# Second attention: where ScalarE applies a chunk's normalization among the copies of one batch

## Chip, cores and metric

One core of one Trainium2 chip runs the whole program as a single launch. The metric is the device time of an execution in microseconds (us); the time before is the median of three runs. All data are 32-bit floats.

## Reference, cut to what matters

The program is a chain of blocks on x of shape 32 x 128 x 128 (batch, token, feature): an attention, a recurrent feed-forward block, a mixture of experts feeding a second attention, and a slot-routing block. The change lies in the second attention. Per batch it computes

```python
# Q, K, V: relu projections of x (128 features = 16 heads of 8)
scores = einsum('bqhd,bkhd->bhqk', Qh, Kh) / sqrt(8)       # + causal mask, key mask
attn = softmax(scores, axis=-1) * query_mask
out = einsum('bhqk,bkhd->bqhd', attn, Vh).reshape(B, T, U) + x
mean, var = out.mean(-1), ((out - mean) ** 2).mean(-1)
normalized = (out - mean) / sqrt(var + 1e-8)
x_next = x_before + gamma * normalized + beta
```

After it, each batch is multiplied with a matrix of its own (a base matrix plus a rank-8 part) and added, and the slot block follows.

## The kernel before, in words

**Engines and order.** Each engine has its own list of instructions, written out by hand by a function of its own (`pe_attend2`, `act_attend2`, `dve_attend2`, `pool_attend2`, `sp_attend2`), and runs it in that order. Engines meet on semaphores alone: an instruction waits until a counter has reached a value. Nothing is reordered by a scheduler.

**Batches, units, chunks.** A batch q (0 to 31, `NB5` = 32) is one sequence of 128 tokens. Its 16 heads are handled as four units u = 4q to 4q+3 of four heads each (`U` = 128 units). A chunk c is four batches (512 tokens), 0 to 7. Each engine's function loops over q, and in iteration q it does, for batch q, the scores; for the four units of batch q-1, the turning of the probabilities; for batch q-2, the product with V. Four kinds of work form the path of a unit u:

- PE `pe_S5(q)` (L2113): 32-row score products of batch q, all 16 heads, into banks 0 to 3. It waits until the maxima of the batch before have read them.
- DVE `dve_max5(u)` (L2122): scale, mask and row maximum of a unit, to one of six buffers.
- POOL `pool_sub5(u)` (L2129): subtract the maximum, 128 x 512.
- ACT `act_exp5(u)` (L2134): exponential in place, 128 x 512.
- PE `pe_T5(u)` (L2141): four transposes of the exponentials into one bank.
- ACT `act_pt5(u)` (L2147): copy of that bank to one of eight buffers.
- PE `pe_PV5(q)` (L2158): 32 products of the turned probabilities with V; it waits for the copies of all four units. ACT `act_o5(q)` (L2165) copies the result, PE `pe_oT(q)` (L2171) turns it back, DVE `dve_norm5(q)` (L2180 to L2187) divides by the sums, POOL `pool_norm5(q)` (L2194) adds x, DVE `dve_stats5(q)` (L2199, L2201) takes mean and variance.

Work of a chunk as a whole stands between these, at hand-chosen steps. A step s runs from 0 to 127, four to each q; `aside(s)` says what belongs to step s, and each engine's loop picks its part of it. For chunk c with finished statistics: `pool_root5` (L2325 to L2330, root and mean on POOL), `act_apply5` (L2336, four activations of 128 x 128 in place, one per batch: scale and shift of the normalization), `pe_gamma5` (L2343, four transposes), `dve_gamma5` (L2349), `pe_select5` and `pe_add5` with their DVE parts. `FINISH` holds the offset of each from `LATE` + 16c; `PROJECT` holds the projections of a later chunk (`act_query5`, L1629, and `act_key5`, L1641, on ACT).

**Banks of PE's outputs.** The turned probabilities of the units ("p"), the product with V ("o") and the query and key projections ("q", "k") share banks 4 and 5 in turn. `plan5` lays the turn down in PE's order, and `pe_drained5` makes an entry wait for the copy of the entry two before it:

```python
        def pe_drained5(key):
            first, n = through5[key]
            if n >= 2:
                pe.wait_ge(*drained5[first][n - 2])
```

With the order of one iteration, "p" 4q-4, "p" 4q-3, "o" q-2, (projection), "p" 4q-2, "p" 4q-1, this means: where there is no projection, `pe_T5(4q-1)` waits for `act_o5(q-2)`; the next iteration's `pe_T5(4q)` and `pe_T5(4q+1)` wait for `act_pt5(4q-2)` and `act_pt5(4q-1)`.

**ScalarE's order.** One iteration of `act_attend2` issues: exp 4q-1, copy 4q-4, copy 4q-3, asides of steps 4q and 4q+1, exp 4q, `act_o5(q-2)`, aside of 4q+2, exp 4q+1, aside of 4q+3, copy 4q-2, exp 4q+2, copy 4q-1. The apply of chunk c stands at step 29 + 16c, in iteration q = 4c + 7, for c = 0 to 6 (chunk 7's stands in `OPENING` of the last stage). POOL does the root of chunk c at the end of its iteration 4c + 6, ahead of `pool_norm5` and `pool_sub5(4q)` of iteration 4c + 7; PE turns the applied chunk (`pe_gamma5`) in iteration 4c + 8. Below, "iteration 7 + 4c" is the iteration of chunk c's apply.

Of the kernel before, what the change touches and what calls it, by code (L numbers as in the profile page):

```python
# [58 lines left out]
def build(nc, xT_d, w_d, out_d):  # L59
# [4 lines left out]
    with ctx:  # L64
# [1928 lines left out]
        LATE = 28  # L1993

        PROJECT = {2: "query", 6: "key", 7: "keysum", 8: "tokens", 11: "masks"}
        FINISH = {0: "root", 1: "apply", 4: "gamma", 14: "select", 18: "add"}

        def aside(s):

# [9 lines left out]
            if s == 26:  # L2009
                yield "b1", 0  # L2010
            for i, what in FINISH.items():
                c, i = divmod(s - LATE - i, 16)
# [10 lines left out]
        def plan_aside(what, c):  # L2023
            if what == "query":
                passes5(("q", c), 4, s_qt, c + 1)
            if what == "key":
                passes5(("k", c), 4, s_kt, c + 1)
            if what == "keysum":
                passes5(("ks", c), 6, s_kx, c + 1)
            if what == "tokens":  # L2030
                passes5(("x", c), 6, s_xc, c + 1)
            if what == "b1":
                passes5("b1", 6, s_b1, 3)
            if what == "factors":
                passes5(("f", c), 6, s_facd, c + 1)
            if what == "gamma":
                passes5(("T", c), 6, s_fd, 3 * c + 1)
            if what == "select":
                passes5(("A", c), 6, s_fd, 3 * c + 2)
            if what == "add":  # L2040
                passes5(("B", c), 6, s_fd, 3 * c + 3)
# [15 lines left out]
        def plan5():  # L2057
# [26 lines left out]
            plan_aside("add", 6)  # L2084
            for what in FINISH.values():
                plan_aside(what, 7)
# [1158 lines left out]
```

## Time and profile before

| | |
|---|---|
| runs, us | 955.38, 953.97, 954.27 (median 954.27) |
| the profiled execution, us | 953.82 |
| its span, us | 952.2 |
| outside the span, us | 1.6 |
| mean granted clock of PE | 0.996 |
| second attention, from its first scores to its last copy | about 645 to 865 us of the span |

Times in the rows are microseconds from the start of the span. PE is TensorE's products, PEld its weight loads, DVE VectorE, ACT ScalarE, POOL GpSimd. L2336 is line 2336 of the kernel. A row of a timeline merges neighbouring instructions of one line ("x4"): start, time from the first start to the last end, engine, line, operation, tiles, and in brackets how long the engine had been idle and which instruction released it. Instructions of one engine overlap a little in the records, so that the next one's start lies before the recorded end; idle time is counted from that end. PB are PE's output banks, AR_s the working area that holds all tiles of this stage.

### The profile page before, as it was taken

To read this page: it belongs to the slowest core of one execution; us is meant where nothing else is said; L and a number is where in the kernel's file an instruction comes from. 1 tells how busy PE (TensorE), PEld (TensorE's weight loads), DVE (VectorE), ACT (ScalarE), POOL (GpSimd) and SP (SyncE) were. 2 spreads that over 40 slices of the span, in tenths; PEclk is the share of its full clock that TensorE was granted. 3 is DMA by queue.
4 is the path that set the end of the run, shared out by engine and by line. 5 is a ranking of instruction groups with operands and counts; after the bars stand their busy time and mean duration, and the time that the engine had idled before them with its cause. 6 is when DMAs were issued, how large, how long until landed. Compare 5 with 4: busy or idle time off the path is not lost.

```text
span 952.2 us, 25813 instructions
## 1 busy us (share of the span) xinstructions
PE 914.9 (96%) x8641; PEld 733.2 (77%) x8641; DVE 790.5 (83%) x3563; ACT 794.7 (83%) x2162; POOL 547.2 (57%) x670
## 2 busy tenths in 40 slices
PE   8999999999999999999989999999989999999887
PEld 7899989898989989963326888867877777775566
DVE  6766989989898989989996767658889889896985
ACT  7998989898989888867875989987788888886886
POOL 4444636464564646442795157757789888891041
PEclk9999999999999999999999999999999999999899
DMA  9100000000000000000236898911000000000002
GB/s 370 71 2 2 2 2 2 2 2 2 1 2 2 2 1 2 2 2 0 91 134 193 275 318 288 328 49 32 24 20 18 24 17 21 24 3 1 2 1 89
DMA packets 36226, 57.70 MB, mean 61 GB/s; under 512 B 3456, under 2 KB 27264, under 8 KB 35712
## 3 DMA queue, kind: packets, MB, share of 16 engines
q1 hardware_dynamic: 36096, 56.07, 17.4%
q8 instruction: 69, 1.13, 0.5%
q14 instruction: 61, 0.50, 0.2%
HBM read 40.85 MB, written 11.01 MB: 54 GB/s over the span
## 4 chain that ended last, share of the span: by engine, by line
PE 54%; DVE 18%; ACT 7%; issue 4%; POOL 3%; DMA 1%; SPq 1%; DVEq 0%; ACTq 0%; POOLq 0%
PE PB L2141 6%; PE PB L270 4%; PE PB L271 4%; PE PB L272 4%; PE PB L437 3%; PE PB L2113 3%; PE PB L2158 3%; PE PB L390 2%; PE PB L459 2%; DVE W L400 2%; PE PB L1423 2%; DVE AR_s L349 2%; PE PB L1425 2%; PE PB L1424 2%; DVE HFXT L607 2%
## 5 line engine op out<-in xcount | busy, mean ns | idle before, releaser
L409 ACT ACTIVATE W<-W,small 128x128 f32<-128x128 f32 x384 | 149.1, 392 | 12.1 <-DVE small L400 11.3
L421 POOL TENSOR_TENSOR W<-W,small 128x512 f32<-128x512 f32 x96 | 100.6, 1053 | 100.2 <-DVE small L415 100.2
L270 PE MATMUL PB<-RR_s 128*128 128x256 f32 (+1 forms) x468 | 151.7, 324 | 5.7 <-DVE RR_s L471 3.8
L271 PE MATMUL PB<-RR_s 128*128 128x256 f32 (+1 forms) x468 | 139.9, 299 | 0.0
L272 PE MATMUL PB<-RR_s 128*128 128x256 f32 (+1 forms) x468 | 139.7, 298 | 0.0
L2129 POOL TENSOR_TENSOR AR_s<-AR_s,small 128x512 f32<-128x512 f32 x128 | 129.8, 1043 | 15.6 <-DVE small L2122 15.5
L2122 DVE CUSTOM_DVE_ANT_0 AR_s<-PB,W 128x128 f32<-128x128 f32 x512 | 111.3, 287 | 2.2 <-PE PB L2113 0.3
L1399 DVE TENSOR_TENSOR RR_s<-AR_s,RR_s 128x512 fp32r<-128x512 f32 (+1 forms) x96 | 65.5, 687 | 44.6 <-ACT RR_s L1392 40.8
L270 PEld LDWEIGHTS PB<-RR_s 128*128 128x128 f32 x468 | 88.8, 190 | 16.0 <-DVE RR_s L471 6.4
L400 DVE CUSTOM_DVE_ANT_0 W<-PB,W 128x128 f32<-128x128 f32 x384 | 86.0, 282 | 13.6 <-PE PB L390 12.8
L349 DVE COPY AR_s<-PB 128x512 f32<-128x512 f32 x128 | 84.8, 682 | 13.2 <-PE PB L272 13.1
L271 PEld LDWEIGHTS PB<-RR_s 128*128 128x128 f32 x468 | 89.1, 190 | 3.4 <-issue 0.7
L272 PEld LDWEIGHTS PB<-RR_s 128*128 128x128 f32 x468 | 88.8, 190 | 3.0
L2134 ACT ACTIVATE AR_s<-AR_s 128x512 f32<-128x512 f32 x128 | 79.7, 625 | 10.6 <-POOL AR_s L2129 10.1
L2147 ACT ACTIVATE AR_s<-PB 128x512 f32<-128x512 f32 x128 | 72.5, 592 | 17.9 <-PE PB L2141 17.6
L443 ACT ACTIVATE HFXT<-PB 128x512 f32<-128x512 f32 x123 | 73.0, 594 | 14.4 <-PE PB L437 11.0
L2141 PEld LDWEIGHTS PB<-W,AR_s 128*128 128x128 f32 x512 | 56.5, 141 | 26.5 <-issue 12.3
L2141 PE MATMUL PB<-W,AR_s 128*128 128x128 f32 x512 | 70.9, 278 | 5.2 <-ACT AR_s L2165 2.7
L1457 POOL TENSOR_TENSOR HFXT<-HFXT,AR_s 128x128 f32 x68 | 41.1, 633 | 56.8 <-DVE AR_s L1447 56.7
L409 ACT ACTIVATION_READ_ACCUMULATOR W<-W,small 128x1 f32 x384 | 73.3, 191 | 0.0
L390 PE MATMUL PB<-AR_s 64*128 64x128 f32 x1024 | 65.8, 278 | 0.0
L1392 ACT ACTIVATE RR_s<-AR_s 128x512 fp32r<-128x512 f32 (+1 forms) x96 | 57.3, 597 | 8.5
(461 smaller groups left out, 2637.6 us busy)
## 6 DMA issues: line engine op xcount, KB each, us to landing
RR_s<-W1D SPq DMA_DIRECT2D x13, 512.0 KB, 4.2
RR_s<-W2D SPq DMA_DIRECT2D x13, 512.0 KB, 4.6
W<-in_w SPq DMA_DIRECT2D x1, 5895.5 KB, 24.3
RR_s<-XD SPq DMA_DIRECT2D x46, 128.0 KB, 3.1
XD<-RR_s SPq DMA_DIRECT2D x18, 256.0 KB, 3.6
HQ<-W1D SPq DMA_DIRECT2D x6, 512.0 KB, 4.3
HQ<-W2D SPq DMA_DIRECT2D x6, 512.0 KB, 4.9
HQ<-XD SPq DMA_DIRECT2D x22, 128.0 KB, 3.5
```

Source lines behind the costliest of these rows:

```text
L270: nc.tensor.matmul(out, lh, rh, start=True, stop=False)
L271: nc.tensor.matmul(out, ll, rh, start=False, stop=False)
L272: return nc.tensor.matmul(out, lh, rl, start=False, stop=True)
L349: nc.vector.tensor_copy(QK[v % 2][pr], bank("k", n)[:, :]).then_inc(s_qk, 1)
L390: mm = nc.tensor.matmul(score(u, h), qk[r, b * 128:b * 128 + 128], qk[r, 256 + b * 128:256 + b * 128 + 128], start=True, stop=True)
L400: nc.vector.tensor_tensor_reduce(SS[r][:, hl], score(u, h), w("mask"), -0.125, 3.0e38, ALU.add, ALU.min, mx[r][:, h:h + 1]).then_inc(s_max, 1)
L409: e = nc.scalar.activation(SS[r][:, hl], SS[r][:, hl], ACTF.Exp, bias=mx[r][:, h:h + 1], scale=-1.0, accum_out=rc[r][:, h:h + 1])
L421: nc.gpsimd.tensor_tensor(s3, s3, over(rc[r], 2, [128, 4, 128]), ALU.mult).then_inc(s_nrm, 1)
L2122: nc.vector.tensor_tensor_reduce(SS5[r][:, hl], score5(u, h), w("mask"), isq8, -3.0e38, ALU.add, ALU.max, mx5[r][:, h:h + 1]).then_inc(s_m ...
L2129: nc.gpsimd.tensor_tensor(s3, s3, over(mx5[r], 2, [128, 4, 128]), ALU.subtract).then_inc(s_sub, 1)
L2134: nc.scalar.activation(SS5[r], SS5[r], ACTF.Exp).then_inc(s_ex5, 1)
L2141: mm = nc.tensor.transpose(bank5(("p", u))[:, hl], SS5[u % 6][:, hl], ident)
```

## The change

The step of "apply" goes from 29 + 16c to 30 + 16c. In `act_attend2` it then falls to the pick at step 4q+2, which stands behind `act_exp5(4q)` and `act_o5(q-2)` of the same iteration and ahead of `act_exp5(4q+1)`. Seven chunks (0 to 6) are touched. No instruction is added or dropped, no wait is changed, no other engine's order changes, and "apply" takes no turn in the banks, so `plan5` lays down the same turns. Chunk 7's apply stays.

```diff
         PROJECT = {2: "query", 6: "key", 7: "keysum", 8: "tokens", 11: "masks"}
-        FINISH = {0: "root", 1: "apply", 4: "gamma", 14: "select", 18: "add"}
+        FINISH = {0: "root", 2: "apply", 4: "gamma", 14: "select", 18: "add"}
```

## Rows read from the trace of the kernel before

**Rows 1.** Page, busy us (share of the span) and instructions
```profile
PE 914.9 (96%) x8641; PEld 733.2 (77%) x8641; DVE 790.5 (83%) x3563; ACT 794.7 (83%) x2162; POOL 547.2 (57%) x670
```

**Rows 2.** Stretches: bounds, length, busy us per engine, granted clock, DMA
```profile
720.50:747.00 26.50, 25.86 (x365) 20.00 (x364) 23.64 (x164) 22.58 (x45) 23.02 (x33) 1.00 0.09 22
```

**Rows 3.** Timeline of PE: start, us, engine, line, what, count, [idle <-releaser]
```profile
697.40 0.65 PE L2141 MATMUL PB<-W,AR_s 128*128 128x128 f32 x4 [1.92 <-ACT AR_s L2165]
...
699.53 1.09 PE L2141 MATMUL PB<-W,AR_s 128*128 128x128 f32 x8
...
726.05 1.09 PE L2141 MATMUL PB<-W,AR_s 128*128 128x128 f32 x8
726.98 0.60 PE L2343 MATMUL PB<-W,AR_s 128*128 128x128 f32 x4
...
727.73 1.08 PE L2158 MATMUL PB<-AR_s 128*32 128x128 f32 x32
...
835.72 0.66 PE L2141 MATMUL PB<-W,AR_s 128*128 128x128 f32 x4 [0.32 <-ACT AR_s L2165]
...
841.38 0.66 PE L2141 MATMUL PB<-W,AR_s 128*128 128x128 f32 x4 [0.44 <-ACT AR_s L2165]
...
853.69 1.29 PE L2141 MATMUL PB<-W,AR_s 128*128 128x128 f32 x8
```

**Rows 4.** Timeline of ACT, round the apply of chunks 0 and 1
```profile
694.70 1.65 ACT L2336 ACTIVATE AR_s<-AR_s,small 128x128 f32<-128x128 f32 x4 [0.54 <-POOL small L2330]
696.25 0.61 ACT L2134 ACTIVATE AR_s<-AR_s 128x512 f32<-128x512 f32 x1
...
698.77 0.58 ACT L2147 ACTIVATE AR_s<-PB 128x512 f32<-128x512 f32 x1
...
721.22 1.65 ACT L2336 ACTIVATE AR_s<-AR_s,small 128x128 f32<-128x128 f32 x4 [0.19 <-POOL small L2330]
722.78 0.61 ACT L2134 ACTIVATE AR_s<-AR_s 128x512 f32<-128x512 f32 x1
723.30 0.57 ACT L2165 ACTIVATE AR_s<-PB 128x512 f32<-128x512 f32 x1
723.77 0.62 ACT L2134 ACTIVATE AR_s<-AR_s 128x512 f32<-128x512 f32 x1
...
725.29 0.58 ACT L2147 ACTIVATE AR_s<-PB 128x512 f32<-128x512 f32 x1
...
728.39 0.63 ACT L2134 ACTIVATE AR_s<-AR_s 128x512 f32<-128x512 f32 x1 [0.56 <-POOL AR_s L2129]
```

**Rows 5.** Timeline of POOL, the subtraction (L2129) behind the root
```profile
695.03 1.04 POOL L2129 TENSOR_TENSOR AR_s<-AR_s,small 128x512 f32<-128x512 f32 x1
...
721.55 1.04 POOL L2129 TENSOR_TENSOR AR_s<-AR_s,small 128x512 f32<-128x512 f32 x1
...
727.31 1.05 POOL L2129 TENSOR_TENSOR AR_s<-AR_s,small 128x512 f32<-128x512 f32 x1 [0.43 <-DVE small L2122]
...
851.95 4.05 POOL L2129 TENSOR_TENSOR AR_s<-AR_s,small 128x512 f32<-128x512 f32 x4
```

**Rows 6.** Waits, 640 to 880: total us, times, longest us
```profile
DVE small L2180 <- PE PB L2171: 15.5, 23, 1.2
...
ACT AR_s L2336 <- POOL small L2330: 5.6, 8, 3.8
...
PE PB L2141 <- ACT AR_s L2165: 2.7, 3, 1.9
```

**Rows 7.** Busy time by stretch, two stretches in the closing stage
```profile
890.00:894.30 4.30, 4.30 (x24) 3.40 (x21) 3.67 (x23) 1.85 (x6) 0.00 (x0) 0.50 0.00 0
894.30:900.00 5.70, 5.22 (x37) 3.42 (x36) 5.27 (x31) 4.95 (x14) 0.00 (x0) 1.00 0.00 0
```

**Rows 8.** Timeline of PE in the closing stage, L2649 twice
```profile
889.24 1.99 PE L2649 MATMUL PB<-AR_s 128*64 128x129 f32 x16
...
896.62 1.10 PE L2649 MATMUL PB<-AR_s 128*64 128x129 f32 x16 [0.48 <-ACT AR_s L2631]
```

## The prediction, made before the changed kernel ran

> **What bounds the kernel now.** First the page's busy times: PE is busy for 96% of the span, every other engine for less [rows 1]. That is an average, so next the stretches round the applies. The applies of chunks 0 to 4 start 26.5 us apart, and the stretch of one such period shows PE busy 25.86 of 26.50 us, POOL 23.02, ACT 22.58, at a granted clock of 1.00; the three periods behind it repeat these figures [rows 2]. PE is therefore the bound of this stage, and whatever stops PE here is paid in full, since its list has nothing to catch up with. Third, PE's timeline: the reader looks for brackets, stretches in which PE had run dry. Of the transposes L2141 that waited for the copy of the product (`act_o5`, L2165) there are three, 2.7 us together [rows 6]: 1.92 us in iteration 7, where chunk 0's apply stands, and 0.32 and 0.44 us in iterations 28 and 29, where none stands [rows 3]. In iterations 11, 15, 19 and 23 PE does not wait for that copy at all. So what the edit can free at most is seen at once: the stall in iteration 7, once, and some hundredths in iteration 31.
>
> Fourth, ACT and POOL side by side round an apply. ACT is idle when the apply's root comes, 0.54 us at chunk 0 and 0.19 at chunk 1 [rows 4]; over the stage that wait is 5.6 us, of which 3.8 belong to chunk 7, which is not touched [rows 6]. Then it runs the four activations, and takes up exp 4q. POOL in that time adds one batch and subtracts the maximum for exp 4q: 695.03 + 1.04 = 696.07 at chunk 0, 721.55 + 1.04 = 722.59 at chunk 1 [rows 5]; exp 4q starts at 696.25 and 722.78 [rows 4]. **The apply fills a hole**: it runs while exp 4q's operand is still being made, and exp 4q comes only 0.14 us later than it could (0.04 us from POOL's end to ACT's start, as where exp 48 waits for POOL: 727.31 + 1.05, then 728.39 [rows 4, 5]).
>
> **The change, part by part.** It removes and adds no instruction, and touches no DMA and no queue but ACT's. It moves four activations, seven times, behind exp 4q and `act_o5`.
>
> *What comes earlier.* exp 4q and `act_o5` by 0.14 us each, not by the 1.56 us of the apply (721.22 to 722.78 [rows 4]), for POOL's subtraction is late next. Iteration 7: `act_o5` ends 0.14 us earlier, so PE's second half of the transposes starts at about 697.26 instead of 697.40. That only matters if nothing holds PE behind it.
>
> *What comes later.* With chunk 1's times: exp 44 at 722.63, `act_o5` 0.52 later at 723.15 (722.78 to 723.30 [rows 4]), the apply 0.47 later at 723.62, its 1.56 us, exp 45 at 725.18 instead of 723.77. From there ACT's list runs with its old spacing and 1.42 us late: copy 43 starts at 725.29 + 1.42 = 726.71 and ends 0.58 us later, at 727.29 [rows 4]; copy 42, one copy and one exponential (1.00 us) ahead, ends at 726.29.
>
> *Who waits for that.* The next iteration's transposes: T 44 goes to the bank of 42, T 45 to the bank of 43. They ran at 726.05 as eight in a row [rows 3], the second four from about 726.54 (four of its spacings of 0.12 us). With 0.05 us from ACT's end to PE (as 696.77 + 0.57, then 697.40, from the row of L2165 beside [rows 3]), T 44 can start at 726.34, 0.3 us late, and T 45 at 727.34, **0.80 us late**. Behind T 45 stand, on PE, gamma (726.98), a V product, PV (727.73 [rows 3]) and all that follows.
>
> *Is more lost, or some won back?* PV also needs copy 43 (727.29, before 728.53: free) and bank turn of copy 44 (about 728.3: free). `pe_gamma5` needs the apply, now done at 725.3 and used at 727.8: free, covered by 2.5 us; that is the cover of the apply's own lateness. The next batch's subtraction ends at 728.36 [rows 5], ACT comes to it at 728.7, 0.3 late, and `act_o5` then waits for PV anyway. DVE's `dve_gamma5` slips by some 0.4 us, into the hole in which DVE waits for PE at the head of the next iteration (DVE waits for L2171 23 times, 15.5 us [rows 6]). Since DVE, and behind it POOL, take up each iteration from PE's L2171, both slip by the same 0.80 us, and at the next apply the engines stand to each other as before. So the price is not paid once but at each apply.
>
> *Chunk 0:* copy 27 started at 698.77 [rows 4]; 698.77 + 1.41 + 0.58 + 0.05 = 700.81, against T 29 at 699.53 + 0.49 = 700.02 [rows 3]: 0.79 late, and the 0.14 us won ahead of it are swallowed. *Chunks 1 to 4:* 4 x 0.80 = 3.2. *Chunk 5* (iteration 27): 0.80 again, but iterations 28 and 29 have the stalls of 0.32 and 0.44 us, where PE waits for a chain over DVE and POOL that starts ahead of the delay. Of the 0.80 they take up all but what PV itself and `dve_gamma5` carry on, which I put at 0.27. *Chunk 6* (iteration 31): the next transposes come only after the set-up products and a hidden layer, at 857.5, copies 122 and 123 would end at 856.7 and 857.7, and the second is needed by PV at 858.1: nothing lost. exp 124's subtraction ends at 851.95 + 1.04 = 852.99 [rows 5]; the transposes at 853.69 took 1.29 us instead of 1.09, so they held a short wait for `act_o5` [rows 3], which goes: about 0.15 won, leaving 0.12 for chunks 5 and 6 together.
>
> **Sum:** 0.79 + 3.20 + 0.12 = 4.1 us more. The last stage takes it over whole: PE runs on without a gap until 880, where DVE begins to lead, starting from PE's products. Against the profiled execution (953.82, of which 952.2 are the span): 957.9 us. The median of the runs stands 0.45 above that execution: 954.27 + 4.1 = **958.4 us**. Bounds of the price at one apply: 0.3 us, if only T 44's wait counted and T 45 were hidden; 1.42 us, ACT's whole slip, if some further wait had no slack. I take 0.80 since both times in it come from rows a microsecond apart.
>
> **Rivals.** *1. Faster: the stall goes.* Mechanism: `act_o5(5)` is freed of the apply's 1.56 us ahead of it. For it: PE's longest stop of the stage is just this wait [rows 3, 6]. It decides by exp 4q's operand: POOL would have to be done when ACT is free, at about 694.2, not at 696.07; and the copies behind must not bind. Then 1.6 us from iteration 7 and 0.2 from iteration 31 are won: 952.5 us. The rows of POOL speak against it, and ends on POOL are said to be rough, but the same kind of end released ACT within 0.04 us at 728.39. 7%. *2. No change.* The late copies fall into PE's slack. It decides by the 0.64 us of each period in which PE isn't busy: if these were at T 44 and T 45, the price is near nothing, 954.3 us. They are elsewhere (most of it behind the projection's copy in iteration 12). 9%. *3. Half.* DVE and POOL run ahead while PE stands, the next subtraction is early, and ACT's hole shrinks; or only part of the wait counts: 2.1 us, 956.4. Against it: they wait for PE in each iteration. 7%. *4. More.* The stops reach `act_o5` or the projection behind them, near 1.2 us each, five times: 960.3 us. 5%. *5. The clock.* In the closing stage 890 to 894.3 ran at a granted 0.50, the level of 1.2 GHz, its neighbour at 1.00, 2.4 GHz [rows 7]; it had fallen in a part of the stage where PE stops again and again. The same 16 products took 1.99 us at the lower and 1.10 at the higher level [rows 8], some 1.5 us over that whole stretch. If the new stops bring such a fall into this stage, or one more in the last, 1.5 us come on top: 959.9. Against it: the stop of 1.92 us in iteration 7 left the clock at 1.00. 5%.
>
> The Trainium skill speaks for case 5, in "TensorE: Matmul & The Clock Gate", section "Part 4: PE-mode transpose": a transpose does not count as PE being busy in the way a product does. By that rule a stage so full of transposes is near the lower level already, and new stops could tip it: the sum would be 4.1 us and the price of the lower level on top, 959.9. The granted 1.00 of rows 2, with twenty transposes in each iteration of it (`pe_T5`, `pe_oT`), disagrees so far.
>
> That the edit does nothing is no case: ACT's order is its list.
>
> **How the numbers follow.** Forecast 67%, range of its own 957.4 to 959.4 (0.6 to 1.0 us per apply). With the half case at the low end and the added cases at the high end, 956.2 to 960.3 holds 84%. About 0.2% (1.9 us) is what a measurement can tell: slower takes the forecast, 3, 4 and 5, 0.84; same 0.09; faster 0.07.
>
> **What would show it.** In the changed profile: ACT idle before exp 4q for 1.4 us in iterations 7, 11, ... by L2129; `pe_T5` with two brackets, 0.3 and 0.5, by L2147, in iterations 8, 12, 16, 20, 24, 28; applies 27.3 us apart; no 1.92 us stop. I am wrong if exp 4q starts before POOL's recorded end, or if the applies stay 26.5 us apart.

## The result, and the profile after

| | before | changed |
|---|---|---|
| median of 6 runs, us | 954.83 | 958.78 |
| lowest to highest, us | 953.97 to 956.16 | 958.47 to 960.03 |
| profiled execution, us | 953.82 | 958.89 |
| its span, us | 952.2 | 957.6 |

The changed kernel is slower: the ratio of the runs is 1.0038, with a 95% interval of 1.0023 to 1.0053, so 2.2 to 5.1 us. The forecast was 958.4, 4.1 us more. The two profiled executions lie 5.1 us apart. (One of the 17 runs of the kernel before beside experiments 5 to 8 took 1262.23 us at a mean granted clock of 0.653 and is left out of their ratios.)

The page's busy times, where one sees that nothing was added: PE 1.9 us more busy than in [rows 1], ACT 1.4 less, on a span 5.4 us longer. The instruction counts are the same; what grew is mostly PE's idle time, and its 1.9 us of busy time are looked at below.

```profile
PE 916.8 (96%) x8641; PEld 734.5 (77%) x8641; DVE 791.2 (83%) x3563; ACT 793.3 (83%) x2162; POOL 548.0 (57%) x670
```

Next ACT's timeline round chunk 1's apply (columns as in [rows 4]).

```profile
721.29 1.08 ACT L2147 ACTIVATE AR_s<-PB 128x512 f32<-128x512 f32 x2 [0.44 <-PE PB L2141]
723.98 0.63 ACT L2134 ACTIVATE AR_s<-AR_s 128x512 f32<-128x512 f32 x1 [1.60 <-POOL AR_s L2129]
724.51 0.58 ACT L2165 ACTIVATE AR_s<-PB 128x512 f32<-128x512 f32 x1
724.99 1.64 ACT L2336 ACTIVATE AR_s<-AR_s,small 128x128 f32<-128x128 f32 x4
726.53 0.62 ACT L2134 ACTIVATE AR_s<-AR_s 128x512 f32<-128x512 f32 x1
...
728.05 0.58 ACT L2147 ACTIVATE AR_s<-PB 128x512 f32<-128x512 f32 x1
```

And POOL's subtraction for exp 44, the first of four (compare [rows 5]).

```profile
722.90 4.05 POOL L2129 TENSOR_TENSOR AR_s<-AR_s,small 128x512 f32<-128x512 f32 x4
```

This is what the prediction described. ACT ends its two copies at 722.38 and now stands idle for 1.60 us until POOL's first subtraction ends, at 722.90 + 1.04 = 723.94; exp 44 starts 0.04 us later. The apply no longer fills that hole. It comes behind the copy of the product, and copy 43 starts at 728.05, which is 5.15 us after the subtraction's start, where it was 725.29 - 721.55 = 3.74 before [rows 4, 5]: 1.41 us late. Over the stage, the waits by kind (who <- for whom: total, times, longest):

```profile
ACT AR_s L2134 <- POOL AR_s L2129: 18.1, 17, 1.9
...
DVE XF L2349 <- PE PB L2343: 6.4, 8, 2.1
...
PE PB L2141 <- ACT AR_s L2147: 2.9, 10, 0.3
...
PE PB L2141 <- ACT AR_s L2165: 2.4, 3, 1.8
```

ACT waits 18.1 us for the subtraction, where the trace before had 10.1. And PE now waits for L2147, the copies, ten times, twice at each of five applies; before, that row did not exist. PE's timeline, with the places that answer to [rows 3]:

```profile
697.15 0.66 PE L2141 MATMUL PB<-W,AR_s 128*128 128x128 f32 x4 [1.79 <-ACT AR_s L2165]
...
698.17 1.93 PE L2113 MATMUL PB<-KR,QS 32*128 32x128 f32 x32
700.03 1.94 PE L2141 MATMUL PB<-W,AR_s 128*128 128x128 f32 x8
701.79 0.61 PE L2343 MATMUL PB<-W,AR_s 128*128 128x128 f32 x4
...
706.56 1.17 PE L2113 MATMUL PB<-KR,QS 32*128 32x128 f32 x32
...
727.68 0.66 PE L2141 MATMUL PB<-W,AR_s 128*128 128x128 f32 x4 [0.24 <-ACT AR_s L2147]
728.69 0.66 PE L2141 MATMUL PB<-W,AR_s 128*128 128x128 f32 x4 [0.35 <-ACT AR_s L2147]
729.18 0.60 PE L2343 MATMUL PB<-W,AR_s 128*128 128x128 f32 x4
...
841.20 0.66 PE L2141 MATMUL PB<-W,AR_s 128*128 128x128 f32 x4 [0.19 <-ACT AR_s L2165]
...
846.83 0.66 PE L2141 MATMUL PB<-W,AR_s 128*128 128x128 f32 x4 [0.40 <-ACT AR_s L2165]
...
859.14 1.17 PE L2141 MATMUL PB<-W,AR_s 128*128 128x128 f32 x8
```

The stops of 0.24 and 0.35 us stand at the transposes of units 44 and 45, in iteration 12. The second ran 1.01 us after the first, where it followed at once before. The stops by L2165 of 1.92, 0.32 and 0.44 us are 1.79, 0.19 and 0.40 now: little came back, as little was to come. Two rows are new in kind: 698.17 and 700.03, 32 score products in 1.93 us and eight transposes in 1.94 us, where the same work takes 1.17 and 1.09 elsewhere (row 706.56, and row 699.53 of [rows 3]). The stretches say why, and give one whole period of the steady part (columns as in [rows 2]):

```profile
698.20:701.50 3.30, 3.30 (x40) 3.08 (x40) 2.26 (x15) 3.26 (x8) 2.25 (x5) 0.53 0.02 5
...
728.00:755.30 27.30, 26.09 (x366) 19.95 (x364) 23.66 (x164) 22.40 (x44) 22.97 (x33) 1.00 0.09 21
```

PE's granted clock was 0.53 on the mean from 698.2 to 701.5, that is the lower level of 1.2 GHz for nearly all of it, right behind the stop of 1.79 us. In the steady part one period of the applies is 27.35 us; the stretch above, 27.30 us long, has PE busy for 26.09 of it, where it was 25.86 of 26.50 [rows 2].

**Where the time came from.** The starts of gamma's transposes (L2343) mark PE's progress, chunk by chunk; a row of four small products (L2308) at 689.40 (689.28 in the changed kernel), ahead of the first apply, gives the origin. The table holds the distance from one mark to the next.

| stretch of PE's list | before, us | changed, us | difference | forecast |
|---|---|---|---|---|
| origin to gamma 0 | 11.06 | 12.51 | +1.45 | +0.79 |
| gamma 0 to gamma 4, four periods | 106.02 | 109.45 | +3.43 | +3.20 |
| gamma 4 to gamma 5 | 26.49 | 27.35 | +0.86 | +0.80 |
| gamma 5 to gamma 6 | 27.60 | 27.31 | -0.29 | -0.68 |
| gamma 6 to gamma 7 | 13.28 | 13.28 | 0 | 0 |
| sum | 184.45 | 189.90 | +5.45 | +4.1 |

The stage took 5.45 us more, which is all that the span grew by. The medians of the runs lie only 3.95 us apart, and the interval of the timed difference ends at 5.1. Runs of one kernel scatter by 0.7 to 5.3 us from lowest to highest, and part of that arises ahead of this stage: the origin mark lay between 688.57 and 693.24 us in the ten traces of this case. Within the steady part the marks are the finer measure: the four periods agree within 0.03 us in the trace before and within 0.04 in the changed one. At chunk 0 they compare single executions, and there the granted clock differs between them (the trace of the kernel before has no fall in this stage). So the experiments below are read by both, and the sum of the stage with care wherever its first entry holds such a fall.

### The profile page after: what moved, and what is told of

Same layout as the page of the kernel before. It is cut to its first block, busy times and chain, and to the rows that moved or that the text cites. A ratio compares the mean times of both kernels' runs of the same rounds, so it can differ in the third digit from the quotient of the medians.

```text
span 957.6 us, 25813 instructions
## 1 busy us (share of the span) xinstructions
PE 916.8 (96%) x8641; PEld 734.5 (77%) x8641; DVE 791.2 (83%) x3563; ACT 793.3 (83%) x2162; POOL 548.0 (57%) x670
## 4 chain that ended last, share of the span: by engine, by line
PE 49%; DVE 17%; ACT 10%; POOL 7%; issue 5%; DVEq 0%; ACTq 0%; POOLq 0%
PE PB L270 5%; PE PB L271 4%; PE PB L272 4%; PE PB L437 4%; PE PB L2141 3%; POOL AR_s L2129 3%; PE PB L390 3%; PE PB L459 2%; PE PB L2158 2%; DVE W L400 2%; PE PB L1423 2%; PE PB L1425 2%; PE PB L1424 2%; PE PB L2113 2%; ACT W L409 2%
## 5 line engine op out<-in xcount | busy, mean ns | idle before, releaser
L2129 POOL TENSOR_TENSOR AR_s<-AR_s,small 128x512 f32<-128x512 f32 x128 | 129.8, 1043 | 19.7 <-DVE small L2122 19.7
L2134 ACT ACTIVATE AR_s<-AR_s 128x512 f32<-128x512 f32 x128 | 79.9, 626 | 18.5 <-POOL AR_s L2129 18.1
L443 ACT ACTIVATE HFXT<-PB 128x512 f32<-128x512 f32 x123 | 73.1, 594 | 14.5 <-PE PB L437 11.5
L2147 ACT ACTIVATE AR_s<-PB 128x512 f32<-128x512 f32 x128 | 72.5, 592 | 15.0 <-PE PB L2141 14.6
```

The lines of the kernel that those rows point to most:

```text
L2129: nc.gpsimd.tensor_tensor(s3, s3, over(mx5[r], 2, [128, 4, 128]), ALU.subtract).then_inc(s_sub, 1)
L2134: nc.scalar.activation(SS5[r], SS5[r], ACTF.Exp).then_inc(s_ex5, 1)
```

## The experiments

Eight experiments ran, the last of them the changed kernel itself once more. Theory H is the prediction's: the apply filled ACT's hole ahead of exp 4q; once moved, it pushes the two copies behind it past the point where PE needs their banks, anew at each apply. Its rivals were that the cost is paid once ("paid once"), that the apply is late for gamma (G), and that ACT's longer wait is itself the price (W). "Stage" is the distance from the origin mark to gamma 7 in the kernel's trace, less the 184.45 us of the kernel before.

**Experiment 1: chunk 0 alone.**

```diff
             for i, what in FINISH.items():
+                i += what == "apply" and s < LATE + 16
```

(on the kernel before)

> Only chunk 0's apply is moved; chunks 1 to 6 keep the old place. Theory H (the apply filled ACT's hole before exp 4q; moved, the copies behind it are late and PE waits at the two transposes of the next iteration, anew at each apply): 0.8 us over the kernel before, or 1.4 if PE's granted clock falls to half behind the stop of iteration 7 as in the changed kernel's profile; applies of chunks 1 to 4 stay 26.5 us apart. Rival 'paid once' (the move shifts the engines against each other for good): most of the 4 us, 3 to 4 us over the kernel before.

Measured: 954.51 us against 954.31 for the kernel before beside it, ratio 1.0001 (0.9991 to 1.0010). Stage +1.49 us. PE's timeline (lines shifted by one: L2142 is `pe_T5`, L2114 the scores):

```profile
696.44 0.66 PE L2142 MATMUL PB<-W,AR_s 128*128 128x128 f32 x4 [1.79 <-ACT AR_s L2166]
...
697.46 1.92 PE L2114 MATMUL PB<-KR,QS 32*128 32x128 f32 x32
699.31 1.95 PE L2142 MATMUL PB<-W,AR_s 128*128 128x128 f32 x8
...
851.51 1.08 PE L2159 MATMUL PB<-AR_s 128*32 128x128 f32 x32 [0.34 <-ACT AR_s L2148]
```

The applies of chunks 1 to 4 are 26.5 us apart again. From the fourth row, which was at 850.86 us before, against an origin 0.83 us earlier: the 1.48 us lost at chunk 0 are still there at the end, no more and no less. "Paid once" would have 3 to 4 us and is out. The trace shows the larger value of H, with the lower clock (1.92 and 1.95 us for the scores and the transposes); the timed runs show 0.2 us with a bound of 1.0. The two differ by more than I can explain from one trace; part of it lies behind the stage, where this trace spent 3.4 us at the lower clock in place of 6.8. Nor does the trace show the two waits of H at chunk 0: the eight transposes of iteration 8 run without a gap, the copies they need ending at 698.92 and 699.92 us. The 1.48 us are the lower clock's, so this experiment speaks against "paid once", and for a price that is gone wherever the apply is back in its old place, but it has no measure of what late copies cost.

**Experiment 2: behind exp 4q only, ahead of the product's copy.**

```diff
                 act_exp5(4 * q)
+                step_of({"apply": act_apply5}, 4 * q + 1)
                 ...
                     act_o5(q - 2)
```

(on the kernel before, with "apply" taken out of the table of asides)

> All seven applies stand behind exp 4q but still ahead of the copy of the turned outputs' product (act_o5). Theory H: ACT waits for the subtraction as in the changed kernel, and act_o5 comes 1.4 us later than before, so PE waits for it at transpose 4q-1 in the same iteration: 1.4 us per chunk instead of 0.86, about 9 us over the kernel before (8 to 10), and little or no wait for the copies of 4q-2 and 4q-1. Rival G (the price is that the apply itself is late for gamma on PE and DVE): the apply is done 1 us earlier than in the changed kernel, so the price is less than its 4 us.

Measured: 964.62 against 954.31, ratio 1.0104 (1.0084 to 1.0123); stage +11.5. ACT, then PE:

```profile
725.70 0.63 ACT L2134 ACTIVATE AR_s<-AR_s 128x512 f32<-128x512 f32 x1 [1.61 <-POOL AR_s L2129]
726.24 1.63 ACT L2336 ACTIVATE AR_s<-AR_s,small 128x128 f32<-128x128 f32 x4
727.78 0.57 ACT L2165 ACTIVATE AR_s<-PB 128x512 f32<-128x512 f32 x1
```

```profile
728.41 0.66 PE L2141 MATMUL PB<-W,AR_s 128*128 128x128 f32 x4 [1.22 <-ACT AR_s L2165]
...
865.96 0.65 PE L2141 MATMUL PB<-W,AR_s 128*128 128x128 f32 x4 [1.46 <-ACT AR_s L2165]
```

The same hole of 1.6 us, then the apply, and `act_o5` is the late one: PE stops 1.22 us for it at each apply, and not once for a copy. The applies are 27.93 us apart, 1.43 more than before, as H had it; the total of 10.3 us by the medians is a little over the 8 to 10 expected. G is out: counted from exp 4q's start the apply ends at 2.17 us, where it was 2.65 in the changed kernel, so it is 0.48 us earlier (not 1 us, as the expectation had it), and yet the price of a period is 1.43 us in place of 0.86. What was left out of the expectation is the stop of 1.46 us in iteration 31.

**Experiments 3 and 4: the root behind POOL's first subtraction, with either place of the apply.**

```diff
                     pool_sub5(4 * q)
+                    step_of({"root": pool_root5}, 4 * q)
                     pool_sub5(4 * q + 1)
                 ...
-                step_of({"root": pool_root5}, 4 * q + 4)
```

> The changed kernel with POOL's root behind its first subtraction of the iteration (pool_sub5(4q), then root, then pool_sub5(4q+1)). Theory H: exp 4q finds its operand 1.8 us earlier and the long stop of PE in iteration 7 shrinks to 0.3 us or less, but then the apply waits for the root and the copies behind it are late by 0.5 us at the transposes: about 956 us, 2 us over the kernel before and 2 to 3 under the changed one. Rival G: the root and so the apply come 1.1 us later still, so slower than the changed kernel, 960 or more.

> The kernel before (apply ahead of exp 4q) with the same late root on POOL. Theory H: now the apply holds exp 4q and act_o5 instead of filling a hole; act_o5 2.1 us later in a steady iteration, 1.5 us in iteration 7: about 11 us over the kernel before. With this order on POOL the move of the apply would pay 9 us, where with the old order it costs 4. Rival (the move is bad whatever POOL does, because of the order of copies): this kernel stays ahead of e3.

Measured: 959.73 us in the new place (ratio 1.0059, 1.0042 to 1.0077; stage +6.5) and 981.15 in the old one (1.0286, 1.0264 to 1.0308; stage +27.5), beside 954.31. Between the two, the direction is H's: with the root late, moving the apply pays 21 us, while with the root early it costs 4 to 5. Both sizes were missed, and for experiment 3 so was the direction against the changed kernel: H had it 2 to 3 us faster, and it is not (5.4 us over the kernel before, periods of 27.69 us in place of 27.35), with a long stop in iteration 7 of 1.09 us and not 0.3. By its time alone rival G, with "960 or more", came nearer; but G's wait, gamma's transposes for the apply, does not occur on PE in this trace: each of its new stops is for a copy. POOL, ACT and PE of experiment 3:

```profile
720.89 0.46 POOL L2194 TENSOR_TENSOR AR_s<-AR_s 128x128 f32<-128x128 f32 x1 [0.93 <-DVE AR_s L2187]
721.65 1.04 POOL L2129 TENSOR_TENSOR AR_s<-AR_s,small 128x512 f32<-128x512 f32 x1 [0.31 <-DVE small L2122]
```

```profile
722.73 0.63 ACT L2134 ACTIVATE AR_s<-AR_s 128x512 f32<-128x512 f32 x1 [0.99 <-POOL AR_s L2129]
...
724.67 1.65 ACT L2336 ACTIVATE AR_s<-AR_s,small 128x128 f32<-128x128 f32 x4 [0.82 <-POOL small L2330]
```

```profile
727.37 0.66 PE L2141 MATMUL PB<-W,AR_s 128*128 128x128 f32 x4 [0.56 <-ACT AR_s L2147]
728.37 0.66 PE L2141 MATMUL PB<-W,AR_s 128*128 128x128 f32 x4 [0.34 <-ACT AR_s L2147]
```

POOL, freed of the root, now waits 0.93 us for DVE's norm and 0.31 for DVE's maxima before it may subtract. **The root, too, had filled a hole.** Moving it behind the subtraction made that one only 0.6 us earlier relative to ACT's copies (a wait of 0.99 us in place of 1.60), and then the apply waited 0.82 us for the root. So copy 43 starts 7.09 us after the pair of copies ahead of exp 44, against 6.76 in the changed kernel, and the period is 27.69 us. In experiment 4 ACT and PE show:

```profile
727.76 1.65 ACT L2336 ACTIVATE AR_s<-AR_s,small 128x128 f32<-128x128 f32 x4 [2.93 <-POOL small L2330]
```

```profile
730.46 1.12 PE L2141 MATMUL PB<-W,AR_s 128*128 128x128 f32 x4 [2.54 <-ACT AR_s L2165]
731.37 1.06 PE L2171 MATMUL PB<-W,AR_s 128*128 128x128 f32 x4
732.36 1.82 PE L2113 MATMUL PB<-AR_s,W 32*128 32x128 f32 x32
```

ACT waits 2.93 us for the root with everything queued behind it, PE stops 2.54 us at each apply, and the clock is at its lower level behind each such stop (32 scores in 1.82 us): the trace has a stretch of 3.4 us at 0.50 behind each of the six stops. The period is 30.75 us, 4.25 more than before, which is about the stop of 2.54 us and half of the 3.4 us at the lower level (an estimate from these rows, as PE is busy for 3.34 of them): I had counted the later root against an idle POOL and no clock. By the same estimate some 10 of the 21 us between experiments 3 and 4 are the clock's.

**Experiment 5: two activations of the four.** The two others, and with them the normalization of the first two batches of chunks 0 to 6, are left out.

```diff
-            for b in range(4):
+            for b in (range(4) if c == 7 else (2, 3)):
```

> The changed kernel with only two of the four activations of the apply for chunks 0 to 6; the first two batches of those chunks are left unnormalized. Nothing else moves, ACT still waits 1.4 to 1.6 us for the subtraction ahead of exp 4q. Theory H (the price is what the apply adds behind that wait, less the slack of the two transposes): 0.78 us less in front of the copies, so they are late by 0.64 and not 1.42 us, just inside the slack: no stops of PE by L2147, applies 26.5 us apart, 954 us, that is within 1 us of the kernel before and 4 under the changed one. Rival W (the wait of ACT for the subtraction is itself the price): the wait is there in full, so 4 us stay, 958.5.

Measured: 955.25 against 954.89 beside it, ratio 1.0004 (0.9993 to 1.0015); stage +0.39. ACT:

```profile
726.57 0.63 ACT L2134 ACTIVATE AR_s<-AR_s 128x512 f32<-128x512 f32 x1 [1.60 <-POOL AR_s L2129]
727.10 0.58 ACT L2165 ACTIVATE AR_s<-PB 128x512 f32<-128x512 f32 x1
727.58 0.86 ACT L2336 ACTIVATE AR_s<-AR_s,small 128x128 f32<-128x128 f32 x2
728.35 0.61 ACT L2134 ACTIVATE AR_s<-AR_s 128x512 f32<-128x512 f32 x1
...
729.87 0.58 ACT L2147 ACTIVATE AR_s<-PB 128x512 f32<-128x512 f32 x1
```

The wait for the subtraction is there in full, 1.60 us, but PE has no stop by L2147 at all, and the applies are 26.60 us apart. W is out: ACT's waiting costs PE nothing by itself; what stands behind it does. Copy 43 starts 729.87 - 726.53 = 3.34 us after the subtraction's end, against 2.70 before and 4.11 in the changed kernel: it is 0.64 us late, and PE pays 0.1 for it.

**Experiment 6: six activations.**

```diff
             act.wait_ge(s_fl, 4 * c + 4)
+            for b in (0, 1) if c < 7 else ():
+                q = 4 * c + b
+                nc.scalar.activation(place(14592 + 256 * c + 128 * b, 128), cs(LN[c % 2], b, 128), ACTF.Identity, ...)
```

> The changed kernel with six activations in the apply of chunks 0 to 6 (two more, whose results go to an unused place). Theory H: beyond the slack every microsecond is paid in full, so each of the two activations of 0.385 us costs PE 0.77 us per chunk together: transposes stop 1.6 us per apply instead of 0.86, applies 28.1 us apart, about 5 us over the changed kernel, 964 us. Rival W: unchanged, 958.8.

Measured: 963.44 against 954.89, ratio 1.0094 (1.0078 to 1.0111); stage +11.9. This trace has 6.8 us at the lower clock from 698.3 us on, and the stage's sum holds it: 2.0 us up to gamma 0, and 29.57 us for the next period where the following ones take 28.12. PE, in iteration 16:

```profile
758.29 0.66 PE L2141 MATMUL PB<-W,AR_s 128*128 128x128 f32 x4 [0.99 <-ACT AR_s L2147]
759.29 0.66 PE L2141 MATMUL PB<-W,AR_s 128*128 128x128 f32 x4 [0.35 <-ACT AR_s L2147]
```

The applies are 28.12 us apart. So the period is 26.60, 27.35 and 28.12 us with two, four and six activations, of which each pair is 0.77 us: the first pair falls for the most part into the slack, and the second and the third cost PE 0.75 and 0.77 us. The copies are late by 0.64, 1.41 and 2.18 us and PE by 0.10, 0.86 and 1.62, so that the slack at the second group of transposes is about 0.55 us in all three.

**Experiment 7: the apply behind the copies.**

```diff
                     act_pt5(4 * q - 1)
+                step_of({"apply": act_apply5}, 4 * q + 2)
```

(on the changed kernel, with "apply" taken out of the table of asides)

> The apply stands at the very end of ACT's iteration, behind the copies of 4q-2 and 4q-1. Theory H: the two stops of PE by L2147 at the transposes go. What is late next: gamma's transposes, which need the apply (0.3 us), and the product with V, whose bank needs the copy of 4q, now behind the apply (0.4 us): about 0.65 us per chunk, applies 27.15 us apart, 957 to 958.5 us. Rival G (the apply's lateness for gamma is the price in the changed kernel): the apply is now 2 us later still, so the price grows to over 2 us per chunk, 966 or more.

Measured: 957.90 against 954.89, ratio 1.0036 (1.0024 to 1.0049); stage +4.7, of which 1.4 up to gamma 0, where the clock was at its lower level again. PE in iteration 12:

```profile
727.54 1.09 PE L2141 MATMUL PB<-W,AR_s 128*128 128x128 f32 x8
728.95 0.63 PE L2343 MATMUL PB<-W,AR_s 128*128 128x128 f32 x4 [0.31 <-ACT AR_s L2336]
729.41 0.39 PE L2207 MATMUL PB<-W,HFXT 128*128 128x128 f32 x2
729.95 1.08 PE L2158 MATMUL PB<-AR_s 128*32 128x128 f32 x32 [0.15 <-ACT AR_s L2147]
```

The eight transposes run through in 1.09 us again. In their stead gamma waits 0.31 us for the apply and the product with V 0.15 for a copy; the applies are 27.22 us apart. H's next-in-line waits are the ones that came, and the period is 0.72 us longer than before, where H had 0.65. G is out here too: the apply is later than in the changed kernel, and the price is lower. Each of the three places behind exp 4q that were tried costs something; with the apply in the hole ahead of it, PE has no stop in iterations 11 and 12 but the one for the projection (L1629), which all of these kernels have.

**Experiment 8: the changed kernel again.**

> The changed kernel once more, beside the others: 4 to 4.5 us over the kernel before. It tells whether PE's granted clock falls to half behind the stop of iteration 7 again: if so, chunk 0's gamma is 1.45 us late and the other chunks' 0.86 each, if not, chunk 0's too is 0.8 to 0.9.

Measured: 959.06 against 954.89, ratio 1.0053 (1.0034 to 1.0072); stage +5.4, with 12.48 us from the origin to gamma 0 (12.51 above) and the same stops in the same places:

```profile
756.72 0.65 PE L2141 MATMUL PB<-W,AR_s 128*128 128x128 f32 x4 [0.23 <-ACT AR_s L2147]
757.72 0.66 PE L2141 MATMUL PB<-W,AR_s 128*128 128x128 f32 x4 [0.35 <-ACT AR_s L2147]
```

The clock was at the lower level again in iteration 8. Together with the first comparison the move costs about 4 to 5 us (3.95 and 4.17 by the medians, 3.6 and 5.1 by the ratios).

## Why the prediction was right, and which terms were off

- **The hole.** The prediction read from [rows 4, 5] that the apply ran while POOL was still making exp 4q's operand, so that exp 4q would gain 0.14 us and not 1.56. Measured: exp 4q starts 0.04 us after the subtraction, and the stop of 1.92 us only shrank to 1.79. Right.
- **The copies.** Forecast late by 1.42 us; measured 1.41. Right.
- **The two stops of PE.** Forecast 0.3 and 0.5 us in iterations 8, 12, ..., 28; measured 0.24 and 0.35 as recorded idle time, in 12, 16, 20, 24 and 28; idle time is counted from the modelled end of the products before, and by the starts, counted from the start of the iteration's 32 scores, T 44 comes at 1.41 us in place of 1.11 and T 45 at 2.42 in place of 1.60, so 0.3 and 0.8 us late. Right in place and kind in these five; in iteration 8 neither stop came (see chunk 0). Experiments 5 and 6 show that the length of the apply behind the wait is what is paid, past 0.55 us of slack, and experiment 2 that the waits move to `act_o5` when the apply stands ahead of it.
- **The price per apply.** Forecast 0.80, measured 0.86 (27.35 against 26.49). The term left out that a group of four transposes takes PE longer right behind a stop: gamma's follow the second group's start by 729.18 - 728.69 = 0.49 us, where the second four of eight in a row take 0.44 (726.54 to 726.98 before).
- **Anew each time.** Right: four periods alike, and experiment 1 took the price away wherever the move was undone.
- **Chunks 5 and 6.** Forecast 0.12 together, measured 0.86 - 0.29 = 0.57. This is the step that was off. It held that the stops in iterations 28 and 29, of 0.32 and 0.44 us, would take up most of the delay, since the chain over DVE starts ahead of it. It put 0.53 us on them; by the starts of PE's rows they took up 0.14 in iteration 28 and 0.03 in iteration 29, and iteration 31 gave back 0.12 where 0.15 was forecast. In iteration 28 the chain over DVE and POOL is indeed ready early, but another one ends last in its place: `act_o5` waits for PE's own product with V, which is as late as PE is.

```profile
840.55 0.60 ACT L2165 ACTIVATE AR_s<-PB 128x512 f32<-128x512 f32 x1 [0.50 <-PE PB L2158]
```

Some 0.19 us of the stop therefore stays however late PE comes: it is 0.18 or 0.19 in experiments 3, 6, 7 and 8 as well, whose delays differ. In iteration 29 almost nothing is taken up (0.40 us of stop left of 0.44): that chain starts with DVE's maxima of batch 29, and these wait for the scores, which stand in PE's list behind the late transposes. The trace has the first maximum 0.41 us after the norm's last step there, where it was 0.20; this reading of iteration 29 was not tested by a run. `dve_gamma5` was late as well; DVE's waits for L2343 grew from 3.7 to 6.4 us.
- **Chunk 0.** Forecast 0.79, measured 1.45 in one trace and 1.42 in the next, and not by the mechanism forecast. ACT's copy 27 came late as forecast:

```profile
700.05 0.58 ACT L2147 ACTIVATE AR_s<-PB 128x512 f32<-128x512 f32 x1
```

But PE, at the lower clock behind the stop of 1.79 us, was slower still: its first four transposes started at 700.03, 0.40 us after copy 26's end, and the second four at 700.94, 0.31 after copy 27's, without a gap between. From one start to the next the scores took 1.86 us in place of 1.11 and the eight transposes 1.76 in place of 0.93; less the 0.13 us won at the stop that is the whole 1.45. Experiment 7, where these copies are not late, has 1.44 up to gamma 0 as well. That was the fifth rival, held at 5% with a price of 1.5 us on top of the 4.1; it came in place of chunk 0's 0.79 and not on top of it. What had spoken against it, that the stop of 1.92 us had left the clock at 1.00, did not carry over: one trace without a fall is no rule.

So mechanism, sign and size hold for the steady part. By the stage's marks the sum came out at 5.4 us, not 4.1: 0.3 from the price per apply, 0.4 from the stretch of iterations 28 to 31, 0.66 from chunk 0. That the medians gave 3.95 us, so close to the 4.1, is in part luck: two terms of the sum were too small, and chunk 0's stood for a wait that did not come.

What stays open is what chunk 0 costs in the timed runs. Those of experiment 1 bound it at 1.0 us where the trace has 1.5, and in each of the seven traces with a fall in iteration 8 (the changed kernel twice, experiments 1, 2, 4, 6 and 7) the stage's difference is above that of the medians, by 0.7 to 3.4 us; without a fall it is above by 1.1 us in experiment 3 and equal in experiment 5 (0.39 and 0.36). The comparison rests on one trace of the kernel before, which has no fall there. Each timed run has its mean granted clock on record, but not where it fell: in 33 runs of the kernel before it was 0.998 in nine, 0.996 in fourteen and 0.995 or 0.993 in ten, with medians of 953.2, 954.6 and 955.7 us; in the twelve of the changed kernel it was never 0.998. So the time at the lower level differs from run to run in both kernels, and of these 45 those with least of it are all the kernel before's; a part of the trace's 1.45 us can be a difference between two executions and not between two kernels. No version faster than the kernel before was found; experiment 3, the one that was to shorten PE's long stop, shows that the root fills a hole on POOL as the apply does on ACT, and that DVE's list is what is late behind both.

## What to carry to other kernels

An instruction that stands just ahead of one which must wait anyway is free as far as it is done when that wait ends (here it ran over by 0.14 us); before moving it, look for what it covers, not only for what it delays. The gain is bounded by when the next operand is there, and the price is the instruction's full length for everything that is queued behind the new place, less the slack of the tightest reader. Where a pattern repeats, compare periods between marks in the bounding engine's list: 0.1 us per period can be read there, when the timed runs scatter by 1 to 5 us. Check the granted clock of each stretch that is compared: a stretch of 3.4 us at the lower level was worth about 1.5 us here, more than the price of a period, and it came in some executions of a kernel and not in others.

## What was not expected of the hardware

PE's granted clock fell from 2.4 to 1.2 GHz for 3.4 us or more after stops of 1.79 to 1.80 us in iteration 7 in five traces (the changed kernel twice, experiments 1, 6 and 7), after the 3.35 us of experiment 2 and the 4.45 of experiment 4; it did not after 1.92 us in the kernel before, 1.81 in experiment 5 and 1.09 in experiment 3. Stops of nearly one length went either way, so what decides is not the length of the stop alone. The five stops of 2.54 us in experiment 4 were each followed by a fall, the five of 1.22 us in experiment 2 by none. The Trainium skill, "TensorE: Matmul & The Clock Gate", section "Part 4: PE-mode transpose", has transposes not count as busy in the way products do; here iterations with twenty transposes each ran at 1.00 except behind such a stop, so that they alone don't bring the lower level; whether they help a stop to bring it, no run shows.
